# The routed experts' down product in split fp32r operands instead of fp32

## What is computed

```python
x2 = rmsnorm(hid, ln2_w).reshape(-1, h)
probs = jax.nn.softmax(x2 @ gate_w.T, axis=-1)
top_w, top_i = jax.lax.top_k(probs, TOPK)             # TOPK = 4 of E = 16
top_w = top_w / jnp.sum(top_w, axis=-1, keepdims=True)
gu = jnp.einsum('th,eih->tei', x2, w1)                # gate and up, I = 176 each
act = jax.nn.silu(gu[..., :I]) * gu[..., I:]
down = jnp.einsum('tei,ehi->teh', act, w2)            # the down product
routed = jnp.einsum('te,teh->th', wfull, down)        # weighted by top_w
return hid + (routed + shared).reshape(b, s, h)
```

## Time and profile before

| what | us |
|---|---|
| median of 3 runs | 1220.91 (1219.78 to 1225.69) |
| the profiled execution: its own time | 1221.95 |
| its span in the profile | 1220.2 |
| its clock: mean granted share | 0.99 |
| first input tile asked for, to the last scatter's start | 989.4 to 1178.9 |
| busy over the span: PE, DVE, ACT, POOL | 1160.6, 846.3, 799.6, 580.7 |

### The profile page before, as it was taken

One profiled execution on the slowest core, in us unless ns is written; L12 is line 12 of the kernel. 1 busy time (PEld: TensorE's weight loads), 2 busy tenths in 40 slices (PEclk: granted clock), 3 DMA queues, 4 the chain that ended last, 5 costly groups with the idle time before them and its releaser, 6 DMA issues.

```text
span 1220.2 us, 25017 instructions
## 1 busy us (share of the span) xinstructions
PE 1160.6 (95%) x7868; PEld 988.4 (81%) x7868; DVE 846.3 (69%) x2663; ACT 799.6 (66%) x2069; POOL 580.7 (48%) x844
## 2 busy tenths in 40 slices
PE   6999999899999999999999999999998879999986
PEld 5766566689999989999989999889986769999962
DVE  5778888576677667876677876668865755555535
ACT  3587888677778776778776787777786524444422
POOL 4063655454334444457343466334453446666650
PEclk9999999999999999999999999999999989999998
DMA  8965555256631211213121131211114237777766
GB/s 271 284 190 168 173 175 170 89 176 191 189 114 57 91 51 57 81 53 123 35 69 37 35 109 67 69 36 54 64 54 132 78 112 116 118 119 118 119 110 223
DMA packets 111779, 139.58 MB, mean 114 GB/s; under 512 B 11364, under 2 KB 94820, under 8 KB 111524
## 3 DMA queue, kind: packets, MB, share of 16 engines
q1 hardware_dynamic: 97204, 119.10, 32.2%
q0 software_dynamic: 14448, 18.88, 9.5%
HBM read 63.36 MB, written 61.87 MB: 103 GB/s over the span
## 4 chain that ended last, share of the span: by engine, by line
PE 76%; DVE 8%; ACT 6%; issue 4%; POOL 3%; DMA 2%; SPq 1%; POOLq 0%; ACTq 0%; DVEq 0%
PE bank L1500 56%; PE bank L1742 5%; PE bank L1926 5%; PE bank L1561 2%; DVE bank L1127 2%; PE bank L1597 2%; PE bank L1614 2%; POOL xs_rows L684 1%; PE bank L1604 1%; PE bank L1905 1%; PE bank L1936 1%; ACT pT L842 1%; POOL sum_rows L746 1%; ACT p L966 1%; DVE hs L1358 1%
## 5 line engine op out<-in xcount | busy, mean ns | idle before, releaser
L1127 DVE CUSTOM_DVE_ANT_0 bank<-bank,mask 128x512 f32<-128x512 f32 (+3 forms) x512 | 235.1, 522 | 42.3 <-PE bank L1500 21.6
L957 ACT ACTIVATE p<-bank,stat 128x512 f32<-128x512 f32 (+3 forms) x256 | 131.6, 527 | 127.0 <-DVE stat L1127 127.0
L537 POOL CAST w_hl<-raw_qkv 128x512 fp32r<-128x512 f32 x96 | 58.8, 613 | 301.9 <-DMA raw_qkv<-in_qkvo 154.2
L1500 PE MATMUL bank<-xT,w_hl 128*128 128x512 f32 x768 | 190.3, 396 | 0.0
L1500 PEld LDWEIGHTS bank<-xT,w_hl 128*128 128x128 f32 x768 | 142.2, 188 | 37.1 <-issue 2.0
L746 POOL DMA_INDIRECT sum_rows<-mid,goal x79 | 122.9, 1555 | 70.7 <-DVE mid L1464 68.1
L966 ACT ACTIVATE p<-p,stat 128x512 f32<-128x512 f32 (+3 forms) x256 | 123.1, 553 | 14.7 <-DVE stat L1361 14.7
L538 POOL TENSOR_TENSOR w_hl<-raw_qkv,w_hl 128x512 fp32r<-128x512 f32 x96 | 124.2, 1294 | 7.8
L1383 DVE TENSOR_TENSOR o<-bank,o 128x512 fp32r<-128x512 f32 x64 | 44.2, 690 | 109.4 <-ACT o L973 109.4
L1500 PE MATMUL bank<-pT,v 128*128 128x256 f32 (+2 forms) x576 | 117.1, 348 | 0.0
L1500 PE MATMUL bank<-k,q 128*128 128x512 f32 (+2 forms) x576 | 111.5, 337 | 2.5 <-ACT pT L950 1.7
(11 more groups left out here) (248 smaller groups left out, 2561.3 us busy)
## 6 DMA issues: line engine op xcount, KB each, us to landing
raw_qkv<-in_qkvo SPq DMA_DIRECT2D x32, 768.0 KB, 5.3
xs_rows<-blank SPq DMA_DIRECT2D x32, 520.0 KB, 3.3
xs_rows<-blank SPq DMA_DIRECT2D x5, 2730.0 KB, 14.6
xrow<-xs_rows SPq DMA_DIRECT2D x79, 130.0 KB, 2.5
raw_o<-in_qkvo SPq DMA_DIRECT2D x32, 256.0 KB, 3.6
sum_rows<-blank SPq DMA_DIRECT2D x3, 2176.0 KB, 8.5
stk<-xT SPq DMA_DIRECT2D x96, 64.0 KB
stk<-k_hl SPq DMA_DIRECT2D x96, 64.0 KB
```

Of the source, the lines that this page charges most:

```text
L537: link(pool.tensor_copy(hi, raw))
L957: act.activation(p2[:, n % 2, POFF[qi]:POFF[qi + 1]], s2(t), ACT.Exp, scale=-1.0, bias=stat2[:, 0, n % 2, t:t + 1], accum_out=stat2[:, 1, ...
L1127: return dve.tensor_tensor_reduce(scores, scores, mask[:, TB - scores.shape[1]:], scale=-1.0, scalar=-2.0 * MASKED, op0=ALU.add, op1=ALU.m ...
L1500: ins = pe.matmul(out, a, b, start=start and i == 0, stop=stop and i == len(pairs) - 1, **kw)
```

## The change

The down product is done in split operands. `w2` is held as a high and a low part over the first 128 of an expert's rows (`w2a`, fp32r), and over the last 48 rows as one tile `w2b` whose lower 64 partitions hold the high part and whose upper 64 hold the low part. The product `h` is written by DVE into `hx` with its last 48 columns twice, 64 apart, so that its transpose carries them on both halves of the partitions. `down` becomes five matmuls: three for the 128 rows, and two for the 48 (the high part of `h` against both halves at once, and the low part against the high weights). The high part of the transposed `h` (`ht_hi`) is written by ACT and the low part (`ht_lo`) by DVE. ACT weights the result instead of DVE. The raw weights have to be split now: ACT rounds (`round_a`, `copy_b`), POOL and DVE subtract (`rest_a`, `rest_b`), POOL casts (`round_b`). The last 48 rows of all experts are loaded twice, in 44 transfers by SP (10 to 12 a block), behind a wait for the end of the shared stage.

```diff
+            w2a = sb(late, "w2a", [P, E, 2, D], F32R)
...
+            w2b_raw = sb(loops_raw, "w2b_raw", [P, E, D])
...
+            w2b = sb(loops, "w2b", [P, E, D], F32R)
+            hx = sb(loops, "hx", [P, 2, 2 * P])
+            ht_hi = sb(loops, "ht_hi", [P, 2, 2 * P], F32R)
+            ht_lo = sb(loops, "ht_lo", [P, 2, 2 * P], F32R)
+            xtt = sb(loops, "xtt", [P, 2, 2, D], F32R)
...
+        W2_POOL = (3, 5, 7, 8)
...
+        def pieces_a(q):
+            return [(e, *piece) for e in range(E // B * q, E // B * (q + 1))
+                    for piece in down_pieces(SHI + e * EI, EA)]
+
+        def pieces_b(q):
+            return [(e, src, half * P // 2 + first, m) for e in range(E // B * q, E // B * (q + 1))
+                    for half in range(2) for src, first, m in down_pieces(SHI + e * EI + EA, P // 2)]
+
+        def block_of(q):
+            return slice(E // B * q, E // B * (q + 1))
...
-                for e in range(E // B * q, E // B * (q + 1)):
-                    for h, g, k, p, first, m in down_pieces(e):
-                        sp.dma_start(w2r[first:first + m, e, h, :], moe_d[g, p:p + m, k, 2 * C * P:])\
-                            .then_inc(w2_in[q], 16)
+                for e, src, first, m in pieces_a(q):
+                    sp.dma_start(w2a_raw[first:first + m, e, 1, :], src).then_inc(w2a_in[q], 16)
 
             def load_tile(i):
                 row = sp.value_load(tab[0:1, i:i + 1], min_val=0, max_val=E * CAP)
                 if i >= NX:
                     sp.wait_ge(e_y, i - NX + 1)
-                sp.dma_start(xt[:, i % NX, :], xs_d[ds(row, P), :]).then_inc(e_x[i % NX], 16)
+                    sp.wait_ge(e_goal, i - NX + 1)
...
             load_w2(B - 1)
+            sp.wait_ge(f_dn, SHARED)
+            for q in range(B):
+                for e, src, first, m in pieces_b(q):
+                    sp.dma_start(w2b_raw[first:first + m, e, :], src).then_inc(part_in[q], 16)
...
+            def rest_a(q):
+                own = block_of(q)
+                pool.wait_ge(w2a_round, q + 1)
+                pool.tensor_tensor(w2a[:, own, 1, :], w2a_raw[:, own, 1, :], f32(w2a[:, own, 0, :]), ALU.subtract)\
+                    .then_inc(w2_pool, 1)
+
+            def round_b(q):
+                own = block_of(q)
+                pool.wait_ge(part_in[q], 16 * (1 + len(pieces_b(q))))
+                pool.tensor_copy(w2b[0:P // 2, own, :], w2b_raw[0:P // 2, own, :]).then_inc(w2_pool, 1)
+
             for s in range(1, LO_POOL):
                 shared_lo(s)
+                if s == 4:
+                    rest_a(0)
             for j in range(TPB):
                 send_tile(B - 1, j)
+            rest_a(1)
+            round_b(0)
+            rest_a(2)
+            round_b(1)
+            rest_a(3)
 
             for i in range(NT):
+                if i in (2, 4):
+                    round_b(i // 2 + 1)
+                pool.wait_ge(e_goal, i + 1)
...
+            def round_a(q):
+                own = block_of(q)
+                act.wait_ge(w2a_in[q], 16 * len(pieces_a(q)))
+                act.activation(w2a[:, own, 0, :], w2a_raw[:, own, 1, :], ACT.Copy).then_inc(w2a_round, 1)
+
+            def copy_b(q):
+                act.wait_ge(part_in[q], 16 * (1 + len(pieces_b(q))))
+                if q:
+                    act.wait_ge(w2b_rest, q)
+                act.activation(w2b_hi[P // 2:, :, :], w2b_raw[P // 2:, block_of(q), :], ACT.Copy).then_inc(w2b_copy, 1)
...
+                if s in (4, 9, 10):
+                    round_a((4, 9, 10).index(s))
...
+            copy_b(0)
+            for i in range(NT + 2):
                 if i < NT:
                     act.wait_ge(e_up, i + 1)
                     if i >= 2:
                         act.wait_ge(e_ht, i - 1)
                     act.activation(sl[:, i % 2, :], bank[i % 2][:, 0:EI], ACT.Silu).then_inc(e_silu, 1)
-                if i >= 1:
+                if i >= 2:
+                    m = i - 2
+                    act.wait_ge(e_dn, m + 1)
+                    if m >= NY:
+                        act.wait_ge(y_sent[m % NY], 16 * (m // NY))
+                    act.activation(yt[:, m % NY, :], bank[6 + m % 2][:, 0:D], ACT.Copy,
+                                   scale=xt[:, m % NX, D + 1:D + 2]).then_inc(e_y, 1)
+                if 1 <= i <= NT:
                     act.wait_ge(e_ht, i)
-                    if i >= 3:
-                        act.wait_ge(e_dn, i - 2)
-                    act.activation(ht[:, (i - 1) % 2, :], bank[4 + (i - 1) % 2][0:H2E, 0:2 * P], ACT.Copy).then_inc(e_htc, 1)
+                    act.activation(ht_hi[:, (i - 1) % 2, :], bank[4 + (i - 1) % 2][:, 0:2 * P], ACT.Copy)\
+                       .then_inc(e_htc, 1)
                 if i + 2 < NT:
                     take_x(i + 2)
+                if i == 0:
+                    round_a(B - 1)
+                if i in (1, 4, 7):
+                    copy_b((1, 4, 7).index(i) + 1)
...
+            def rest_b(q):
+                dve.wait_ge(w2b_copy, q + 1)
+                dve.tensor_tensor(w2b[P // 2:, block_of(q), :], w2b_raw[P // 2:, block_of(q), :],
+                                  f32(w2b_hi[P // 2:, :, :]), ALU.subtract).then_inc(w2b_rest, 1)
...
+            rest_b(0)
             for i in range(NT + 2):
                 if i < NT:
                     dve.wait_ge(e_silu, i + 1)
-                    dve.tensor_tensor(sl[:, i % 2, :], sl[:, i % 2, :], bank[i % 2][:, EI:2 * EI], ALU.mult)\
+                    both = [P, 2, EB]
+                    dve.tensor_tensor(hx[:, i % 2, 0:EA], sl[:, i % 2, 0:EA], bank[i % 2][:, EI:EI + EA], ALU.mult)
+                    dve.tensor_tensor(hx[:, i % 2, EA:].rearrange("p (a n) -> p a n", a=2)[:, :, 0:EB],
+                                      sl[:, i % 2, EA:].unsqueeze(1).to_broadcast(both),
+                                      bank[i % 2][:, EI + EA:2 * EI].unsqueeze(1).to_broadcast(both), ALU.mult)\
                        .then_inc(e_h, 1)
                 if i >= 2:
                     m = i - 2
-                    dve.wait_ge(e_dn, m + 1)
                     if m >= NY:
                         dve.wait_ge(y_sent[m % NY], 16 * (m // NY))
                     dve.tensor_tensor(goal[:, m % NY:m % NY + 1], xt[:, m % NX, D:D + 1].bitcast(I32),
-                                      spare[:, :], ALU.min)
-                    dve.tensor_scalar(yt[:, m % NY, :], bank[6 + m % 2][:, 0:D], xt[:, m % NX, D + 1:D + 2], None,
-                                      ALU.mult).then_inc(e_y, 1)
+                                      spare[:, :], ALU.min).then_inc(e_goal, 1)
+                if 1 <= i <= NT:
+                    dve.wait_ge(e_htc, i)
+                    dve.tensor_tensor(ht_lo[:, (i - 1) % 2, :], bank[4 + (i - 1) % 2][:, 0:2 * P],
+                                      f32(ht_hi[:, (i - 1) % 2, :]), ALU.subtract).then_inc(e_htl, 1)
                 if i + 2 < NT:
                     take_x(i + 2)
+                if i in (1, 4, 7):
+                    rest_b((1, 4, 7).index(i) + 1)
...
             def down(i):
                 if i % (E // B) == 0 and i < E:
-                    pe.wait_ge(w2_in[i // (E // B)],
-                               16 * sum(len(list(down_pieces(e))) for e in range(i, i + E // B)))
-                pe.wait_ge(e_htc, i + 1)
+                    pe.wait_ge(w2_pool, W2_POOL[i // (E // B)])
+                    pe.wait_ge(w2b_rest, i // (E // B) + 1)
+                pe.wait_ge(e_htl, i + 1)
                 if i >= 2:
                     pe.wait_ge(e_y, i - 1)
-                for h in range(2):
-                    ins = pe.matmul(bank[6 + i % 2][:, 0:D], ht[:, i % 2, P * h:P * (h + 1)],
-                                    w2r[:, ds(expert[i], 1), h, :].rearrange("p a n -> p (a n)"),
-                                    start=h == 0, stop=h == 1)
-                ins.then_inc(e_dn, 1)
+                first, last = slice(0, EA), slice(EA, 2 * P)
+                a_hi, a_lo = (w2a[:, ds(expert[i], 1), part, :].rearrange("p a n -> p (a n)") for part in (HI, LO))
+                product(bank[6 + i % 2][:, 0:D],
+                        [(ht_hi[:, i % 2, first], a_hi), (ht_lo[:, i % 2, first], a_hi), (ht_hi[:, i % 2, first], a_lo),
+                         (ht_hi[:, i % 2, last], w2b[:, ds(expert[i], 1), :].rearrange("p a n -> p (a n)")),
+                         (ht_lo[0:EB, i % 2, last], w2b[0:EB, ds(expert[i], 1), :].rearrange("p a n -> p (a n)"))])\
+                    .then_inc(e_dn, 1)
 
             def turn_h(i):
                 pe.wait_ge(e_h, i + 1)
                 if i >= 2:
-                    pe.wait_ge(e_htc, i - 1)
+                    pe.wait_ge(e_htl, i - 1)
                 for h in range(2):
-                    ins = pe.transpose(bank[4 + i % 2][0:H2E, P * h:P * (h + 1)], sl[:, i % 2, H2E * h:H2E * (h + 1)],
-                                       ident[:, :])
```

(42 more changed lines are left out.)

22 lines of the change are left out of this document (12 added, 10 removed).

## The result

The changed kernel takes 1264.06 us (median of 4 runs, 1262.66 to 1265.66) against 1221.7 for the kernel before: a ratio of 1.0347, 95% interval 1.0324 to 1.0371. The direction was forecast, the size not: 42 us slower, where 25 were predicted and 36 were the range's end. The profiled execution has a span of 1262.5 us.

What follows compares the result with a forecast made beforehand. The prediction took PE to bound the kernel before and a two-tile latency cycle after. Losses of 15.05 + 2.4 + 1.7 + 1.0 + 4.9 = 25.0 on 1221.95 gave 1247.0, less 1.0 for the median: 1246 us, range 1228 to 1257.

Steps and rivals of the forecast that it cites:

- SP's queue ahead of tile 4: At the loop's start, 39 more transfers at 0.386 us each, all on the path: 15.05 us lost, bounds 11.3 and 17.6.
- The latency from one `down` to the next: Steady loop, through ACT and DVE: release 2.06 us behind `down`'s start; two-tile cycle of 4.65, 2.32 a tile, loses 4.9.
- five take 0.60: In `down`, split matmuls of 256 columns start 0.12 us apart, so five take 0.60 instead of 0.86.
- rule on passes: True fp32 takes 4 passes, so `down`'s five split matmuls would take 0.54 us: pace 1.95; the prediction kept 0.60.
- What stands behind that wait: PE's sequencer after `ht_lo`'s release: `up` starts 1.50 + 0.03 us later, the next `down` 1.05 behind that.
- PE's work: Steady loop: PE's own work falls to 1.05 + 0.60 + 0.36 = 2.01 us a tile, hidden in the 2.32 cycle.
- PE would be busy for 86 to 88%: Sign in the changed profile's steady loop: PE's idle time ahead of `up`, put down to issue, with scatters 2.3 us apart.
- The routing: Ahead of the loop, `rest_a(0)` on POOL holds DVE's ranking of experts; tile 0 and SP's queue come 2.4 us later.
- The clock: After PE's wait ahead of tile 4, the granted clock is low again: 1.7 us lost, bounds 0 and 2.7.
- Weight work inside the loop: Copies and subtractions of `w2b` blocks at i = 4 and 7 make DVE late for `ht_lo`: 1.0 us, bounds 0.5 and 2.
- At nothing: Work taken as covered: `w2a`'s first three blocks, POOL's remaining weight work, block 0 of `w2b`, DVE's multiplies and `ht_lo`, POOL's scatters.
- sum of 25.0: Whole kernel, us lost: 15.05 queue, 2.4 routing, 1.7 clock, 1.0 weight work in the loop, 4.9 loop pace.

Runs made afterwards that it cites:

- e1: Changed kernel with the fifth matmul of `down` on all 128 rows instead of 48: 1255.38 us, ratio 1.0294 to the kernel before.
- e13: Changed kernel with the fifth matmul of `down` on 96 rows instead of 48: 1253.82 us, ratio 1.0281 to the kernel before.
- e10: e1 with the wait in `down` split, three matmuls behind the wait for `ht_hi`, two behind that for `ht_lo`: 1238.84 us.
- e16: Changed kernel with the wait in `down` split between `ht_hi` and `ht_lo`, the fifth matmul left on 48 rows: 1252.73 us.
- e15: Changed kernel with 128-row fifth matmul, split wait, 48-row transfers, weighting on ACT and the start rearranged once more: 1225.17 us, ratio 1.0046 to before.
- e6: Changed kernel with POOL's first subtraction of `w2a`'s blocks moved from amid the shared experts to behind the routed rows' scatters: 1261.63 us.
- e3: Changed kernel with only SP's queue reordered: block 0 of `w2b`, tiles 4 to 7, blocks 1 and 2, tiles 8 and 9, block 3: 1258.22 us.

## Why the prediction was wrong

- **SP's queue ahead of tile 4** is one of two failed steps of about the same size, and in it a term was sized wrong: "39 more x 0.386 = 15.05 us" measured 28.26 - 5.70 = 22.56 (from the start of the first of these transfers to tile 4's), 0.578 each. The mechanism was right; the price came from 12 transfers of `w2r` and even the upper bound of 0.45 was too low. The new ones are at 0.465, and 20 of them at 0.64. 7.5 us.
- **The latency from one `down` to the next**: the form, the cycle over two tiles and the spacing on ACT held. The step that failed is "five take 0.60": taken from a row on 128 rows for a matmul on 48. `down` ended at 1.01, not at 0.76. Pace 2.444 instead of 2.325; the loop lost 13.2 instead of 4.9, 8.3 more. With 128 rows (e1) the numbers of that paragraph are met: 0.60, 2.00, 2.322; with 96 rows (e13) the pace is 2.323. The prediction weighed a rule on passes, and e1's 0.60 is what its own rows gave, not the 0.54 of that rule. What the Trainium skill (TensorEngine Tiling (Array Packing), Key Properties) says of a change of mode it did not weigh.
- **What stands behind that wait**: right, 1.52 from release to `up` against 1.53 (e1), and e10 shows it by taking three matmuls from behind the wait.
- **PE's work** of 2.01 is not contradicted: e16's 2.340 less the 0.09 and 0.19 around the fifth and 0.06 between the transposes behind it (0.28 apart, in e1 0.22) is 2.00. No run has that pace; the best is e15's 2.142. The sign that PE would be busy for 86 to 88% failed, since small gaps don't show: even in e1, at the forecast pace, it shows 48.42 of 50.00 us, 97%.
- **The routing**: the mechanism and its price held (2.4 forecast, 2.26 in the held operation, 2.25 by e6). That tile 0 was asked for 2.35 later is luck, though: 1.37 of it is the lower clock ahead of the routing, and the stretch behind it grew by 0.98 only, because the kernel before had been profiled in the longer of its two lengths. **The clock**: 1.7 forecast, 1.7 measured from tile 4's turn to the second scatter, a stretch that holds more than the clock's effect; behind the wait of 9.46 the windows show 0.51 and then full speed:

```profile
1026.00:1030.10 4.10, 3.92 (x13) 3.24 (x13) 0.95 (x4) 0.70 (x2) 0.00 (x0) 0.51 0.49 129
1030.10:1034.00 3.90, 3.90 (x26) 3.39 (x25) 2.58 (x5) 2.62 (x8) 2.50 (x2) 1.00 0.27 41
```

- **Weight work inside the loop**: 1.0 forecast, 2.1 measured for the 14 intervals as a whole. PE's two waits for `ht_lo` in them, 0.39 and 0.43, are what the forecast described; to what the rest belongs is not shown. **At nothing**: block 0's work was hidden by tile 4's wait, as said, and came out when e3 took that wait away. Not forecast: 2.0 more between the last scatters, where the granted clock fell to 0.50, and 1.6 less behind them, of which the cause is open.

7.5 + 8.3 + 1.1 + 2.0 - 1.6 = 17.3, all of the 17.3 by which the span is beyond the sum of 25.0.
